# Neighbourhood attention on one core: products with V and scores of two tiles taken together in every second step

## What is computed

```python
xn = _layernorm(x, ln1_w, ln1_b)
qkv = xn @ w_qkv + b_qkv
...
kw = _windows(kp, H, W)          # 7 x 7 neighbours, zero padded
vw = _windows(vp, H, W)
attn = jnp.einsum('bnhwd,bnhwdk->bnhwk', q, kw)
attn = attn + rpb[None, :, None, None, :]
attn = jax.nn.softmax(attn, axis=-1)
out = jnp.einsum('bnhwk,bnhwdk->bnhwd', attn, vw)
...
x = x + (out @ w_proj + b_proj)
xn2 = _layernorm(x, ln2_w, ln2_b)
h = jax.nn.gelu(xn2 @ w_fc1 + b_fc1, approximate=False)
x = x + (h @ w_fc2 + b_fc2)
```

## Time and profile before

| | |
|---|---|
| time, median of 3 runs | 1790.41 us (1789.75 to 1790.43) |
| the profiled execution's own time | 1782.08 us |
| its span, first to last instruction | 1779.9 us |
| mean granted TensorE clock | 0.978 |
| busy share PE, PEld | 94%, 75% |
| busy share DVE, ACT, POOL | 74%, 69%, 42% |
| first `scores` to last `out` | 21.4 to 719.0 us |

### The profile page before, as it was taken

One profiled execution on the slowest core, in us unless ns is written; L12 is line 12 of the kernel. 1 busy time (PEld: TensorE's weight loads), 2 busy tenths in 40 slices (PEclk: granted clock), 3 DMA queues, 4 the chain that ended last, 5 costly groups with the idle time before them and its releaser, 6 DMA issues.

```text
span 1779.9 us, 76274 instructions
## 1 busy us (share of the span) xinstructions
PE 1671.3 (94%) x32219; PEld 1341.4 (75%) x32219; DVE 1318.0 (74%) x3852; ACT 1220.4 (69%) x2699; POOL 749.5 (42%) x986
## 2 busy tenths in 40 slices
PE   5899999999999989897899999999999999999896
PEld 3566676666676766797788888888888888888574
DVE  2677788888877776688577777777777777775885
ACT  5788887887877755555676767777777777775232
POOL 6554455655555544121323443334453434530013
PEclk8899999999999998998999999999999999999998
DMA  4432333343332322378514333333333343235775
GB/s 120 118 82 77 101 88 83 89 105 97 87 101 79 97 66 57 101 222 261 190 37 88 79 69 74 65 82 86 64 83 75 59 90 83 64 87 131 176 147 73
DMA packets 278596, 175.12 MB, mean 98 GB/s; under 512 B 92140, under 2 KB 271778, under 8 KB 276660
## 3 DMA queue, kind: packets, MB, share of 16 engines
q1 hardware_dynamic: 262210, 149.42, 30.5%
q0 software_dynamic: 13664, 20.43, 8.1%
q10 hardware_dynamic: 2384, 0.40, 0.1%
HBM read 99.63 MB, written 83.46 MB: 103 GB/s over the span
## 4 chain that ended last, share of the span: by engine, by line
PE 70%; DVE 12%; issue 5%; POOL 5%; ACT 4%; DMA 3%; SPq 2%; DVEq 0%; POOLq 0%; ACTq 0%
PE banks L1402 21%; PE banks L1380 11%; PE banks L1383 10%; PE banks L409 6%; DVE zone L611 4%; PE banks L403 3%; PE banks L368 2%; PE banks L1694 2%; PE banks L358 2%; PE banks L1681 2%; PE banks L416 2%; PE banks L382 2%; DVE st L598 1%; PE banks L456 1%; DVE W L653 1%
## 5 line engine op out<-in xcount | busy, mean ns | idle before, releaser
L1442 DVE COPY Gm<-banks 128x448 f32<-128x448 f32 x896 | 549.0, 637 | 187.7 <-PE banks L1380 111.1
L1421 ACT ACTIVATE Gm<-banks 128x448 f32<-128x448 f32 x896 | 516.3, 625 | 216.8 <-PE banks L1380 157.1
L1402 PE MATMUL banks<-Gm,U 128*32 128x128 f32 x12544 | 515.1, 274 | 9.9 <-POOL U L1497 6.2
L1402 PEld LDWEIGHTS banks<-Gm,U 128*32 128x32 f32 x12544 | 337.9, 110 | 53.6 <-issue 48.3
L1383 PE MATMUL banks<-V,zone 118*32 118x224 bf16 x7040 | 293.2, 259 | 3.5 <-issue 3.5
L873 POOL TENSOR_TENSOR W<-W,mx 128x280 f32<-128x280 f32 x196 | 130.2, 664 | 227.2 <-DVE mx L660 226.8
L1514 POOL DMA_DIRECT2D Yd<-Zd x106 | 81.8, 772 | 331.2 <-DMA Yd<-Zd 284.9
L1380 PE MATMUL banks<-V,zone 118*128 118x224 bf16 x1824 | 216.2, 261 | 1.5 <-issue 0.9
L1383 PEld LDWEIGHTS banks<-V,zone 118*32 118x32 bf16 x7040 | 193.3, 96 | 5.5 <-issue 5.3
L1380 PEld LDWEIGHTS banks<-V,zone 118*128 118x128 bf16 x1824 | 155.9, 98 | 49.9 <-issue 40.7
L523 ACT ACTIVATE W<-W,mx 128x140 f32<-128x140 f32 x392 | 156.2, 402 | 0.3
(11 more groups left out here) (189 smaller groups left out, 2620.6 us busy)
## 6 DMA issues: line engine op xcount, KB each, us to landing
W<-Vd SPq DMA_DIRECT2D x392, 49.0 KB
Yd<-YS SPq DMA_DIRECT2D x28, 448.0 KB, 4.6
Zd<-YS SPq DMA_DIRECT2D x56, 224.0 KB, 5.2
UL<-Ud SPq DMA_DIRECT2D x27, 448.0 KB, 4.5
Yd<-Zd POOLq DMA_DIRECT2D x95, 112.0 KB, 3.3
YL<-Yd SPq DMA_DIRECT2D x40, 196.0 KB
zone<-Mbf SPq DMA_DIRECT2D x28, 256.0 KB
Vd<-W SPq DMA_DIRECT2D x56, 112.0 KB
```

The costliest lines, as they stand in the source:

```text
L1402: ins = e.matmul(p[32 * x:32 * x + 32, :], self.U7[(2 * P + ch) % 3][:, sl, 8 * (3 - q):8 * (3 - q) + 32], self.Gm[:, par, r:r + 2, :], st ...
L1421: e.activation(dst, src, ACT.Copy).then_inc(S["gm_act"], 1)
L1442: v.tensor_copy(dst, src).then_inc(S["gm_dve"], 1)
```

## The change

Steps whose tile number n is odd are paired. `scores` of tiles n - 1 and n, and `out` of tiles n - 7 and n - 6, are all done in the paired step, as out, out, scores, scores behind `turn`; the other steps have neither. `smax` moves from lag 0 to lag 1, in the same place of the step. The even tile's scores go to columns 0 to 139 of banks 2 and 3 and the odd one's to columns 256 to 395. Bank 6 becomes a ring of eight tiles, so that a row of seven can wrap round its end and `row` is then two copies. When the row's last tile is even, `row` stands behind the step's `out`s. `prob`, `inv`, `snorm`, `turn`, `keep` and `v_load` stay at their lags.

```diff
-        order += tile((3, "inv")) + [x for x in kept if x not in done] + tile((7, "row")) + first.get(u, [])
-        order += tile((4, "turn"), (3, "snorm"), (2, "prob"), (6, "out"), (3, "v_load"), (0, "scores"))
+        kept, row = tile((5, "keep")), tile((7, "row"))
+        paired = n % 2 == 1
+        order += tile((3, "inv")) + [x for x in kept if x not in done] + ([] if paired else row) + first.get(u, [])
+        order += tile((4, "turn"), (3, "snorm"), (2, "prob"))
+        if paired:
+            order += tile((7, "out"), (6, "out")) + row + tile((1, "scores"), (0, "scores"))
+        order += tile((3, "v_load"))
...
-        order += parts[:cut] + tile((0, "smax")) + parts[cut:] + fill.get(u, [])
+        order += parts[:cut] + tile((1, "smax")) + parts[cut:] + fill.get(u, [])
...  scores
-                if n:
+                if n and n % 2 == 0:
                     e.wait_ge(S["lmax"], n)
-                at = 448 * i + 64 * x
+                at, to = 448 * i + 64 * x, 256 * (n % 2)
...
-                        ins = e.matmul(self.psum[2 + j][c:c + 32, 0:140], ...
+                        ins = e.matmul(self.psum[2 + j][c:c + 32, to:to + 140], ...
...  out
-                x = n % 7
+                x = n % 8
...
-                if x == 0 and n:
+                if n >= 8 and n % 2 == 0:
                     e.wait_ge(S["orow"], n // 7)
...  row
-                e.wait_ge(S["pv"], n + 1)
+                e.wait_ge(S["pv"], (n | 1) + 1)
...
+                x0 = 7 * r % 8
+                if x0 > 1:
+                    e.activation(to[:, 8 - x0:7], of[:, 0:x0 - 1], ACT.Copy)
+                e.activation(to[:, 0:min(7, 8 - x0)], of[:, x0:min(x0 + 7, 8)], ACT.Copy).then_inc(S["orow"], 1)
...  smax
-                v.wait_ge(S["scores"], n + 1)
+                v.wait_ge(S["scores"], (n | 1) + 1)
```

## The result

The changed kernel takes 1806.38 us, median of 4 runs (1800.31 to 1807.97), against 1790.08 for the kernel before. The ratio is 1.0077, 95% interval [1.0056, 1.0099]: 0.8% slower, where no measurable change was forecast (1791.0, range 1782 to 1800).

A forecast was written before the change was run, and what follows sets the result against it. PE was taken to bound the tile stage's outer stretches and DVE's loop over the gelus the middle. -10.5 (gain) + 10.7 (loss) + 0.4 (`row`) = +0.6 us on 1790.41 gave 1791.0 us, range 1782 to 1800.

The forecast's parts named there:

- the gate: Tile stage: ACT waits at `prob` for DVE's `smax` of the step before, with the gelus behind it; 10.7 us lost.
- 0.4 for `row`: ACT's `row` becomes two copies for 21 of 28 rows; 0.4 us lost, ends 0 and 4.3.
- The hand-over from `prob` to `inv`: DVE's `inv` follows ACT's `prob`; the forecast had no term for a later `prob` delaying it.
- The path now: PE leads from 60 to 260 and 510 to 720 us, DVE's loop over the gelus from 260 to 510.
- The gain: PE's pairs save 0.155 us a tile in changes of form, on 68 tiles of the outer stretches; 10.5 us gained.
- the lost cover: Steps without `out` and `scores` have nothing between two `turn`s, so PE waits for `keep`; the forecast had no term.
- full drain: Each change of form on PE empties the engine; three changes cost 0.52 us, the gain would be 17.6 us.
- The loss: ACT's `prob` waits for a later `smax`, mostly ahead of the gelus in the middle stretch; 10.7 us lost, ends 0 and 12.
- I count 0 beyond the 0.155: PE's other shifts, fills 0.54 later in paired steps and 0.85 earlier in unpaired ones, cost or gain nothing further.
- PE's gain is given back: Rival: DVE or ACT is close behind PE, 2 of 10.5 us arrive and the gelus' wait counts whole; 1799, chance 0.28.
- The change doesn't do what it says: Rival: PE's 0.1 us gaps belong to a new kind of operands, not to the form; 1801, chance 0.07.
- `v_load` a step later: `v_load` of an even tile waits for an `out` one step later, delaying loads behind it; cost 0.

The follow-up runs named there:

- e1: The kernel before with `prob` one step after its `smax` instead of two, no pairs; 1795.81 against 1790.25 us, ratio 1.0047.
- e10: e2 with `prob` one step after its `smax` instead of two; 1792.95 us, ratio 1.0019 to the kernel before.
- e12: The kernel before with `prob` and `inv` each one step earlier, no pairs; 1812.32 us, ratio 1.0155.
- e11: e10 with `inv` also one step earlier, so `smax`, `prob` and `inv` stand in three steps running; 1804.85 us, ratio 1.0107 to the kernel before.
- e7: The changed kernel with out, scores, out, scores alternating in the paired step; 1825.42 us, ratio 1.0197 to the kernel before.
- e2: The kernel before with out and scores pairs in one step, scores taken a step early, `smax` at lag 0; 1785.19 us, ratio 0.9972.
- e14: The changed kernel with `keep` ahead of `prob` in steps without out and scores, only away from the gelus; ratio 1.0041 to the kernel before.
- e5: The kernel before with early scores pairs in even steps and out pairs in odd steps, `smax` at lag 0; 1780.85 us, ratio 0.9961.

## Why the prediction was wrong

Three kernels lead from the kernel before to the changed one. e1 brings the gate, but it also gives everything behind `prob` a step of slack that the kernel before doesn't have. e10 adds the pairs. The changed kernel takes that slack away again. The starts of `keep` of tiles 70 and 140 in e1, and then in e10:

```profile
255.45 0.58 ACT L533 ACTIVATE W<-banks 98x512 f32<-98x512 f32 x1
505.93 0.58 ACT L533 ACTIVATE W<-banks 98x512 f32<-98x512 f32 x1
```

```profile
255.47 0.59 ACT L539 ACTIVATE W<-banks 98x512 f32<-98x512 f32 x1
509.30 0.58 ACT L539 ACTIVATE W<-banks 98x512 f32<-98x512 f32 x1
```

With the last `out`s of the table these give, in us of the tile stage (a plus is slower):

| | to tile 70 | to tile 140 | behind | whole | by the ratios | forecast |
|---|---|---|---|---|---|---|
| the gate: e1 less before | +2.3 | +6.8 | +0.3 | +9.4 | +8.4 | +10.7 |
| the pairs: e10 less e1 | 0.0 | +3.4 | -8.2 | -4.8 | -5.0 | -10.5 |
| the slack behind `prob` gone: changed less e10 | +5.7 | -2.0 | +1.5 | +5.2 | +10.4 | 0 |
| changed less before | +8.1 | +8.1 | -6.4 | +9.8 | +13.8 | +0.2, and 0.4 for `row` |

Over e12 and e11 the same way goes +22.4 (gate without the slack), -6.0 (pairs) and -6.6. By either way the changed kernel loses 14.6 to 15.8 us beside what the pairs gain, where 10.7 was forecast.

Two steps of the prediction failed: the share of the pairs' gain that reaches the end, and the hand-over from `prob` to `inv`, which was put at nothing.

**The path now**: half right. DVE leads in the middle stretch, with its loop closing over the gelus; e1 lost 6.8 of its 9.4 us there. But "there a shorter PE shortens the kernel" did not hold in the first stretch.

**The gain, 10.5 us from fewer changes of form**: this is the first step that failed. A change costs 0.15 us (e7), not 0.10, and yet only half of the 10.5 arrived. Three comparisons differ in the pairs alone: e2 less before gives -5.3 us, e10 less e1 -4.8, e11 less e12 -6.0. The prediction took PE's shares of the chain as the share of the saving that arrives, 34 tiles or 5.3 us in the first stretch and as much in the last. In the first the three comparisons gain 1.4, 0.0 and 1.6 us, in the middle they lose 3.8, 3.4 and 1.2, and only in the last do they gain, 7.7, 8.2 and 5.6. Why so little comes in the first stretch is not shown. PE's wait at `turn` for `keep` grows there with the pairs, from 8.0 to 9.5 us (before to e2) and from 12.3 to 16.9 (e12 to e11), so the lost cover is a candidate for a part of it.
The block itself was mis-read by less. The second `out` in the changed kernel adds 0.23 (147.20 to 147.79, less 0.36), not 0.25, and the second `scores` 0.23, not 0.29: I had taken the spacing inside a block as what a next block of the same form would have, and it is shorter. At 0.15 each, three changes cost 0.45; that is an estimate, since the one between `turn` and `out` was not measured apart. The Trainium skill ("TensorEngine Tiling (Array Packing)", Key Properties) says that changing the tiling mode drains the engine. The 0.52 that the prediction worked out for a full drain was nearer to this 0.45 than its own 0.31.

**The loss, 10.7 us, "`smax` a step later, `prob` not"**: right for what it priced, ACT's wait at `prob`. With slack behind `prob` the gate costs 9.4 us in the tile stage (e1), 8.4 by the ratios, and nearly as the working had it by stretches: 2.3, 6.8 and 0.3 us against 1.7, 8.3 and 0.7. That the changed kernel's middle stretch lost 8.1 where 8.3 was forecast is in part luck, since the pairs lost there too and the table's third row gives some back.

**The hand-over from `prob` to `inv`, put at nothing**: this is the second step that failed. `inv` stays at its lag, one step behind `prob`, and the prediction priced only what ACT waits for at `prob`. It gave no price to DVE waiting at `inv`, the first event of the next step, for that later `prob`. DVE's wait there is 17.0 us from 60 to 260 us in the changed kernel, 7.9 before and none in e1. Moved alone, `inv` one step behind the gated `prob` costs 13.0 us (e12 less e1) and 11.8 (e11 less e10), 8.6 and 7.1 of them in the first stretch. From e10 to the changed kernel, where `snorm`, `turn` and what follows close up too, it is 5.2 us by the traces and 10.4 by the ratios, with 5.7 in the first stretch. How much of that is `inv` is not shown, since e11 ends 6.6 us after the changed kernel.

**"I count 0 beyond the 0.155"**: not right. The steps without `out` and `scores` let `turn` run into `keep`: 34.5 us of waits instead of 10.3, and the middle stretch loses 1.2 to 3.8 us with the pairs. e14 takes back 2.4 us of the changed kernel's loss, or 6.4 by the ratios, by moving `keep`.

**The rivals.** The one on the slower side had 1799, "PE's gain is given back" because DVE or ACT is close behind. In the first stretch the gain did not arrive, which fits it; over the whole stage half did. The time is beyond it because of the hand-over that no rival named. "The change doesn't do what it says" falls by e7. `row` in two parts, `v_load` a step later and `m_proj` were not tried apart. `row`'s wait for the `out`s, which the prediction took as nothing, is 3.9 us of ACT's time in the changed kernel. Nor was the clock tried, see the last section.

## What to carry to other kernels

Moving a stage by one step in a software pipeline over in-order engines moves every hand-over behind it: list all of them, from the moved stage to the first one that keeps its old distance, and price the chain DVE, ACT, DVE as a whole, not the one place where something critical stands behind the wait. A share of the chain of waits doesn't say how much of a shorter instruction arrives: here two stretches had the same share, one gained almost nothing and the other more than its share. Pair up work for the sake of TensorE's forms by taking the first stage early, not the later ones late (e2 and e5 are 0.3 and 0.4% faster than before, the changed kernel 0.8% slower), and look at the cover that the emptied steps lose.

## What was not expected of the hardware

A change between the full array, 32-column tiles and 32 x 32 tiles costs about 0.15 us each in this mix (0.30 us for two, read off a block of 64 matmuls that is otherwise the same), and the tile stage grows by 0.134 us for each (26.2 us over 196 more changes; by the ratios 21 us, 0.11 each).

In e12, TensorE had been idle for 1.6 of 4.5 us, when `scores` waited 0.69 for `smax` and `turn` 1.03 for `keep`, and ran the next 3.9 us at a mean granted clock of 0.56. Windows: length, busy PE, PEld, DVE, ACT, POOL, then the clock:

```profile
144.00:148.50 4.50, 2.87 (x51) 2.23 (x49) 4.50 (x15) 3.08 (x9) 3.15 (x4) 1.00 0.00 0
148.50:152.40 3.90, 3.82 (x45) 2.89 (x46) 2.80 (x17) 1.70 (x6) 1.36 (x3) 0.56 0.47 121
```

That is close to the lower of its two levels (1.2 of 2.4 GHz), and m_cov's eight matmuls (L416) take 1.81 us in it, where they take 1.16 in the kernel before. One wait of about a microsecond was so followed by a loss of another 0.65.

The clock is also not quite the same in the two kernels. Windows of 510 to 720 us, before, and then after, with the clock third from the end:

```profile
510.00:720.00 210.00, 195.44 (x2574) 140.27 (x2566) 146.22 (x659) 136.21 (x358) 102.55 (x141) 0.94 0.29 79
```

```profile
510.00:720.00 210.00, 189.29 (x2694) 140.77 (x2695) 153.98 (x705) 145.23 (x388) 107.02 (x150) 0.98 0.31 83
```

In the first two stretches it is 0.98 and 1.00 in both, so it doesn't explain what was lost there. In the last one the changed kernel had the higher clock, so a part of the 6.4 us that it gave back may be the clock's. It isn't all: e12 and e11 have 0.97 both from 510 to 715 us, and the pairs gain 5.6 us there.
